# A second combine with a home for every tile's rows, summed on TensorE through diagonals of the weights

## The reference, cut to what matters

```
# expert FFN (64 experts, 6 chosen per token, at most 64 tokens per expert; later ones are dropped)
scores = softmax(xf @ gate_w.T);  topk_w, topk_idx = top_k(scores, 6)
eo = (silu(g) * u) @ down_proj * buf_w;  routed[token] += eo;  x = x + 0.5 * (routed + shared)
# wave FFN, on layernorm(x)
amp = sigmoid(x @ amp_w + amp_b);  ph = tanh(x @ ph_w + ph_b) * pi
h = (cos(ph) + sin(ph)) * amp
for l in range(2):
    e = h @ ent_w[l] + ent_b[l];  ent = e @ ent_pw[l] + ent_pb[l]
    h = layer_norm(h + ent, ln3_g[l], ln3_b[l])
    t = h @ path_w[l] + path_b[l]                    # two paths
    mod = cos(phase[l]) + sin(phase[l])
    h = layer_norm(h + sum over paths of t * mod, ln4_g[l], ln4_b[l])
```

## Time and profile before

| | us |
|---|---|
| median of 3 runs | 786.45 (785.43 to 788.97) |
| profiled execution | 787.34 |
| its span | 785.7 |
| PE / DVE / ACT / POOL busy | 577.7 / 389.2 / 233.4 / 295.2 |
| 48 gathers of the second combine (L1610), POOL busy | 51.3 |
| input wave's products (L1814), PE | in groups of 4 tiles |

### The profile page before, as it was taken

The page is one execution under the profiler, slowest core; times in us unless marked ns, Lnnn a source line. Parts: engine busy times, 40 slices in busy tenths (PEclk is TensorE's granted clock), DMA queues, the critical chain, the costliest instruction groups (busy, mean ns, idle before and its releaser), DMA issues. The chain is left out here.

```text
span 785.7 us, 10359 instructions
## 1 busy us (share of the span) xinstructions
PE 577.7 (74%) x3486; PEld 368.9 (47%) x3486; DVE 389.2 (50%) x1102; ACT 233.4 (30%) x638; POOL 295.2 (38%) x383
## 2 busy tenths in 40 slices
PE   2666259970799999998953398984336697897796
PEld 1334125530466666665632254564213586554485
DVE  4656213333475676855442033366758547624135
ACT  1222024440132232321310144420033463142664
POOL 0556611106601537160326012257754266003065
PEclk9757569995799999998985599987577798998899
DMA  8886048842200314340166168733370000000001
GB/s 322 290 295 215 16 129 271 282 164 80 73 9 1 81 41 85 35 170 4 37 241 138 55 211 301 243 104 98 89 80 1 0 1 1 1 1 0 2 1 53
DMA packets 39723, 82.96 MB, mean 106 GB/s; under 512 B 7805, under 2 KB 27906, under 8 KB 38816
## 3 DMA queue, kind: packets, MB, share of 16 engines
q1 hardware_dynamic: 26144, 45.03, 17.7%
q0 software_dynamic: 13248, 37.07, 17.2%
q10 hardware_dynamic: 288, 0.30, 0.1%
HBM read 60.21 MB, written 26.35 MB: 110 GB/s over the span
## 5 line engine op out<-in xcount | busy, mean ns | idle before, releaser
L434 POOL DMA_INDIRECT expert_in<-xn_sent,scatter_slots x72 | 70.9, 985 | 79.7 <-DVE slots L383 50.5
L770 DVE SCALAR_TENSOR_TENSOR work<-work,banks 128x96 f32<-128x96 f32 x64 | 16.3, 254 | 124.1 <-ACT work L750 124.1
L1845 PE MATMUL banks<-w_gu,w_dn 128*128 128x256 f32 x256 | 68.4, 394 | 0.0
L1610 POOL DMA_INDIRECT w_dn<-expert_out,slots x48 | 51.3, 1069 | 26.4 <-issue 14.2
L790 PE MATMUL banks<-ident,work 128*128 128x128 f32 x128 | 29.5, 316 | 42.6 <-DMA work<-expert_in 42.6
L1251 POOL DMA_INDIRECT w_gu<-expert_out,gather_slots x48 | 49.3, 1028 | 28.7 <-DVE gather_slots L1259 14.7
L799 PE MATMUL banks<-w_gu,work 128*64 128x192 f32 x512 | 58.5, 352 | 0.0
L1968 POOL TENSOR_TENSOR var_eps<-mv,eps 128x1 f32<-128x1 f32 (+1 forms) x70 | 13.7, 195 | 116.8 <-ACT w_dn L1894 55.2
L1845 PEld LDWEIGHTS banks<-w_gu,w_dn 128*128 128x128 f32 x256 | 46.0, 199 | 4.2
L790 PEld LDWEIGHTS banks<-ident,work 128*128 128x128 f32 x128 | 13.8, 149 | 67.5 <-issue 41.5
L1970 POOL TENSOR_TENSOR rstd<-var_eps,minus_half 128x1 f32<-128x1 f32 (+1 forms) x70 | 42.4, 606 | 5.5
(11 more groups left out here) (271 smaller groups left out, 1258.0 us busy)
## 6 DMA issues: line engine op xcount, KB each, us to landing
work<-expert_in SPq DMA_DIRECT2D x64, 128.0 KB, 3.8
expert_out<-work SPq DMA_DIRECT2D x64, 128.0 KB, 3.8
w_gu<-in_gate_up SPq DMA_DIRECT2D x10, 768.0 KB
w_gu<-in_gate_up POOLq DMA_DIRECT2D x6, 768.0 KB, 5.6
expert_in<-w_dn SPq DMA_DIRECT2D x4, 1024.0 KB, 7.5
w_dn<-in_down SPq DMA_DIRECT2D x10, 384.0 KB
w_gu<-in_gate_up SPq DMA_DIRECT2D x1, 3840.0 KB, 12.0
w_dn<-in_down SPq DMA_DIRECT2D x1, 3072.0 KB, 25.8
```

The source lines that it names most:

```text
L434: nc.gpsimd.indirect_dma_start(out=m.expert_in, out_offset=bass.IndirectOffsetOnAxis(m.scatter_slots[u][:, at:at + 1], 0), in_=xn[:, t, :] ...
L1610: nc.gpsimd.indirect_dma_start(out=w.combined[q % 2][:, t * TOPK + k, :], out_offset=None, in_=m.expert_out, in_offset=bass.IndirectOffset ...
L1845: last = nc.tensor.matmul(f.p_lin[t % DEEP], f.uT[t % DEEP][:, c, :], w.lin[:, step, c, :], start=(step > 0 and c == 0), stop=(c == KC - 1))
```

## The change

Every tile has a home for its 6 x 256 gathered columns (`w.combined`, eight places; tile 7 takes tile 0's), so gathers no longer wait for a buffer's combine. ACT makes a diagonal matrix of each tile's weights for each choice (8 places), PE sums the six products of diagonal and rows into PSUM bank 2 or 3, and DVE adds the bank to `m.x`. `fold_phase` and `last_phase` become one block. The input wave runs in groups of tiles 0 to 3, 4 and 5, 6 and 7 (`FIRST_NORM`), each with its own root on POOL: the first behind the gathers of tile 5, the second behind those of tile 6, the third at the end. `finish_maps` and the attention's weights (`finish_qkv`) move ahead of the last tiles. The phases are reduced by POOL in the second expert stage (`phases_to_turns`, ahead of `load_last_weights`), with two loads of its own. The first wave's transpositions use two banks, so a transposition waits for the copy of the tile two before it; the wait is there in the second wave too.

```diff
@@ experts_phase, call 1, POOL @@
+                phases_to_turns(nc, m, a, pool, x.out, before)
                 for part, groups_used in enumerate((2, 3, 4, 6), 1):
+def phases_to_turns(nc, m, a, pool, s_out, before):
...
+    pool.dma_start(w.phase, a["rows"][:, first:first + NL * PW * D].broadcast_to([P, NL * PW * D])).then_inc(m.s_phase, 16)
+    pool.dma_start(w.ent_b.rearrange("p a b -> p (a b)"), a["ent_b"]).then_inc(m.s_phase, 16)
+    pool.wait_ge(m.s_phase, 32)
...
+    for l in range(NL):
...
+        chain(nc.gpsimd.tensor_scalar(turns, phase, 0.5 / PI, big, ALU.mult, ALU.add))
+        chain(nc.gpsimd.tensor_scalar(whole, turns, -big, None, ALU.add))
+        for part in (c1, c2):
+            chain(nc.gpsimd.tensor_scalar(turns, whole, -part, None, ALU.mult))
+            chain(nc.gpsimd.tensor_tensor(phase, phase, turns, ALU.add))
+        chain(nc.gpsimd.tensor_scalar(turns, phase, TURN_PI, -TURN_PI, ALU.min, ALU.max))
+    pool.wait_ge(s_out, before + RING)
+    for l in range(NL):
+        chain(nc.gpsimd.tensor_copy(w.ent_b_wide[:, l], w.ent_b[:, l, :].unsqueeze(2).broadcast_to([P, EW // P, P])))
@@ finish_maps, on DVE @@
     split_bias(nc, m, w, chain)
+    meanwhile()
     for k in range(1, STEPS):
         eng.wait_ge(s_last, k)
...
+def fold_pool(nc, m, w, s, wave, pool):
+    last_row = pool.to_reg(SLOTS + P - 1)
+    for t in range(TILES):
+        if t == 6:
+            pool.wait_ge(s.sin, 2 * NL)
+        if t == 7:
+            pool.wait_ge(s.summed, 1)
+        for k in range(TOPK):
+            nc.gpsimd.indirect_dma_start(
...
+                bounds_check=last_row, oob_is_err=False).then_inc(s.gathered[t], 16)
+        if t == 5:
+            norm_roots_pool(nc, m, wave, pool, 0, [0])
+        if t == 6:
+            norm_roots_pool(nc, m, wave, pool, 0, [1])
+    norm_roots_pool(nc, m, wave, pool, 0, [2])
+def fold_scalar(nc, m, w, f, s, wave, act):
+    def diagonals(t):
+        for k in range(TOPK):
...
+            nc.scalar.activation(w.diag[j % DIAGS], m.ident[:, :], ACT.Copy, scale=m.weights[:, t, k:k + 1]
+                                 ).then_inc(s.diag, 1)
...
+    for t in range(5):
+        diagonals(t)
+    wave_scalar_x(nc, w, f, wave, act, 0, range(0, 4))
+    diagonals(5)
+    wave_scalar_x(nc, w, f, wave, act, 0, range(4, 6))
+    diagonals(6)
+    diagonals(7)
+    wave_scalar_x(nc, w, f, wave, act, 0, range(6, 8))
+def fold_vector(nc, m, w, f, s, wave, dve, chain):
+    def add_sum(t):
+        dve.wait_ge(s.summed, t + 1)
+        chain(nc.vector.tensor_tensor(m.x[:, t, :], m.x[:, t, :], m.banks[:, 2 + t % 2, 0:D], ALU.add))
+        dve.sem_inc(s.added, 1)
...
+    add_sum(0)
+    add_sum(1)
...
+    finish_maps(nc, m, w, dve, chain, s.maps, s.scaled, s.last_steps, lambda: (add_sum(2), add_sum(3)))
+    stats_all_vector(nc, m, wave, chain, range(0, 4))
+    apply_all_vector(nc, m, f, wave, dve, 0, range(0, 4))
+    add_sum(4)
+    add_sum(5)
+    stats_all_vector(nc, m, wave, chain, range(4, 6))
+    dve.wait_ge(s.small, 4 * 16)
+    finish_qkv(nc, w, chain)
+    apply_all_vector(nc, m, f, wave, dve, 0, range(4, 6))
+    for t in range(6, 8):
+        add_sum(t)
+        stats_all_vector(nc, m, wave, chain, range(t, t + 1))
+    apply_all_vector(nc, m, f, wave, dve, 0, range(6, 8))
+def fold_tensor(nc, m, w, f, s, wave, pe):
+    def sum_tile(t):
+        if t >= 1:
+            pe.wait_ge(s.added, t)
+        for k in range(TOPK):
...
+            pe.wait_ge(s.diag, j + 1)
+            last = nc.tensor.matmul(m.banks[:, 2 + t % 2, 0:D], w.diag[j % DIAGS], w.combined[t][:, k, :],
+                                    start=(k == 0), stop=(k == TOPK - 1))
...
+    pe.wait_ge(s.halved, 1)
+    nc.tensor.matmul(m.banks[:, 3, :], w.last_row, w.amp_ph[:, KC - 1, :], start=True, stop=True).then_inc(s.last, 1)
+    pe.wait_ge(m.s_ent, 16 * 2 * NL)
...
+    sum_tile(0)
+    sum_tile(1)
+    for k in range(1, STEPS):
+        step_shift(k)
+    sum_tile(2)
+    sum_tile(3)
+    pe.wait_ge(s.scaled, 1)
...
+    sum_tile(4)
+    wave_tensor_x(nc, m, w, f, wave, pe, 0, range(0, 4), f.p_turn_x)
+    sum_tile(5)
+    wave_tensor_x(nc, m, w, f, wave, pe, 0, range(4, 6), f.p_turn_x)
+    sum_tile(6)
+    sum_tile(7)
+    wave_tensor_x(nc, m, w, f, wave, pe, 0, range(6, 8), f.p_turn_x)
@@ wave_tensor_x @@
         if p < tiles.stop:
+            if p >= 2:
+                eng.wait_ge(s.xT, norms * TILES + (p - 1))
```

More of the change, by code:

```diff
@@ L1477, in last_weights @@
     w.parts = [g[:, first:first + 128].bitcast(BF16) for first in (8192, 8960, 3072)]
-    w.combined = [flat(d, 10240 + 3072 * b, (TB * TOPK, D)) for b in range(2)]
+    one = TOPK * D
+    homes = [d[:, 10240 + one * b:10240 + one * (b + 1)] for b in range(4)]
+    homes += [m.work[:, 0:one], m.work[:, one:2 * one], m.w_qkv[:, :, :].rearrange("p c n -> p (c n)"), homes[0]]
+    w.combined = [home.rearrange("p (k d) -> p k d", d=D) for home in homes]
+    spare = m.w_qkv[:, :, :].rearrange("p c n -> p (c n)")
+    w.phase = spare[:, 0:NL * PW * D]
+    w.turns = [spare[:, 2 * PW * D:3 * PW * D], m.w_proj[:, :, :].rearrange("p c n -> p (c n)")]
+    w.cos_turns = [tile[:, :, :].rearrange("p t d -> p (t d)") for tile in (m.xn, m.xn_sent)]
+    w.ent_b = flat(m.w_sgu[:, :, :].rearrange("p c n -> p (c n)"), 0, (NL, EW // P))
     return w
@@ new lines, with __init__ @@
+class Fold:
+    def __init__(self, sem):
+        self.small = sem("small_last_weights_loaded")
+        self.prod, self.read = sem("fold_product_ready"), sem("fold_products_read")
+        self.wide = sem("bias_columns_spread")
+        self.halved, self.last = sem("amplitude_map_halved"), sem("last_row_of_input_maps_ready")
+        self.abs, self.sin, self.half = sem("phase_sizes_ready"), sem("phase_sines_ready"), sem("half_pi_made")
+        self.gathered = [sem(f"last_rows_gathered_tile{t}") for t in range(TILES)]
+        self.diag, self.used = sem("weight_diagonal_ready"), sem("weight_diagonal_used")
+        self.summed, self.added = sem("tile_summed"), sem("tile_sum_added")
+        self.maps, self.scaled, self.last_steps = sem("step_maps_ready"), sem("step_maps_scaled"), sem("last_row_of_step_maps_ready")
@@ new lines, in fold_scalar @@
+def fold_scalar(nc, m, w, f, s, wave, act):
+    def diagonals(t):
+        for k in range(TOPK):
+            j = t * TOPK + k
+            if j >= DIAGS:
+                last_used = j - DIAGS
+                if last_used % TOPK == TOPK - 1:
+                    act.wait_ge(s.summed, last_used // TOPK + 1)
+                else:
+                    act.wait_ge(s.used, last_used - last_used // TOPK + 1)
+            nc.scalar.activation(w.diag[j % DIAGS], m.ident[:, :], ACT.Copy, scale=m.weights[:, t, k:k + 1]
+                                 ).then_inc(s.diag, 1)
+    for l in range(NL):
+        nc.scalar.activation(w.cos_turns[l], w.turns[l], ACT.Abs).then_inc(s.abs, 1)
+    act.wait_ge(s.half, 1)
+    act.wait_ge(s.abs, NL)
+    for l in range(NL):
+        both = slice(l * PW, (l + 1) * PW)
+        nc.scalar.activation(w.phase_sin[:, both].rearrange("p a b -> p (a b)"), w.turns[l], ACT.Sin).then_inc(s.sin, 1)
+        nc.scalar.activation(w.phase_cos[:, both].rearrange("p a b -> p (a b)"), w.cos_turns[l], ACT.Sin, scale=-1.0,
+                             bias=w.half_pi).then_inc(s.sin, 1)
+    for t in range(5):
[6 more added lines that the diff above has]
+    wave_scalar_x(nc, w, f, wave, act, 0, range(6, 8))
@@ L2044, in _ @@
         def _(pe):
-            def last_rows():
-                pe.wait_ge(s_scaled, 1)
-                pe.wait_ge(wave.tanh, TILES)
-                for k in range(1, STEPS):
-                    nc.tensor.matmul(m.banks[:, 4 + k, 0:D], w.last_row, w.lin[:, k, KC - 1, :], start=True, stop=True
-                                     ).then_inc(s_last, 1)
-            wave_tensor(nc, m, w, f, wave, pe, 0, s_maps, REST, last_rows)
+            fold_tensor(nc, m, w, f, fold, wave, pe)
+            wave_tensor(nc, m, w, f, wave, pe, 0, fold.maps)
             for t in range(TILES):
```

337 lines of the change are left out of this document (140 added, 197 removed).

## The result

The changed kernel takes 800.38 us (median of 8 runs, 793.41 to 811.82) against 788.04 (785.43 to 789.34) for the kernel before on the same chip: 1.0128 times the time [1.0095, 1.0162]. The forecast of 788.0, with a range to 793.5, was wrong. Besides being slower, it scatters: 18 us from lowest to highest where before scatters by 4. Its mean granted clock was 0.874 in the run of 793.41 us and 0.841 in that of 811.82.

What follows compares the result with a forecast made beforehand. Bound: the stretch from 516 to 616 us, where no engine is busy throughout and POOL's gather issues are the backbone. Terms +0.3 (first step), +0.4 (second wave), +0.9 (crowded loads) gave +1.6: 788.0 on the median, range 780.5 to 793.5.

Steps and rivals of the forecast that it cites:

- Phases: Second expert stage: POOL's arithmetic takes up to 20 us, moves the first load 0 to 5 us; crowding costs 0.9.
- The loads crowd: Rival, chance 0.23: the first megabyte load comes at 466 with the second, the expert stage loses some 4 more: 792.
- an expert stage longer by over 2 us: Sign of being wrong: the expert stage takes over 2 us longer than in the kernel before.
- The load at the start: New 512 KB load, starting with the second expert stage: lands some 5.2 us later, POOL free between 446 and 466.
- Maps ready: DVE's step maps in the fold: 15.2 us in all, done at 566.4.
- the first root: POOL's root ahead of tile 6's gathers: waits for statistics at 568.1, POOL idle 1 to 2 us before it.
- sum 5: Tile 5's sum on TensorE: comes behind the wave of tiles 0 to 3, which ends at 582.3.
- the gathers of tile 7: POOL, behind the second root: issued from about 588, the sixth at 595.4, landed at 599.4.
- first step: First transposition of the steps on TensorE, end of the fold: 616.1 against 615.77 before.
- The gate: First root stands in POOL's program ahead of tile 6's gathers and waits for 568.1, with 12 gathers queued behind it.
- The clock stays high: Rival, chance 0.26: idle stretches do not lower TensorE's clock, the four-tile wave takes 10.2 instead of 12.5: -6.5, 781.5.
- Gathers starve: Rival, chance 0.10: DVE's scalings lengthen the first 36 gathers by at most 4 us, ending at 570.7: 790.6.

Runs made afterwards that it cites:

- the repeat: The changed kernel measured once more, unedited: 799.73 us, 1.0164 times the kernel before.
- e1: Changed kernel with POOL's 16 phase instructions dealt out between the loads of the last weights: 791.98 us, 1.0073 times the kernel before.
- e8: e1 with POOL's 512 KB load held until the second expert stage's second pair is out: 787.2 us, 1.0015 times the kernel before.
- e6: e5 with the second root of the input wave behind tile 7's gathers in POOL's program: 789.87 us, 1.0029 times the kernel before.
- e7: e5 with tile 5's sum ahead of one six-tile wave, tiles 4 and 5 normalised before the attention fold: 780.8 us, 0.9922 times before.
- e11: Changed kernel with the 512 KB load held until the second pair is out, arithmetic left in one block: 794.74 us, 1.0128 times before.
- e2: Kernel before, with POOL waiting until the second expert stage's 12th pair ahead of the first load of last weights: 792.26 us, 1.0089.
- e5: Changed kernel with phase reductions and spreads back on DVE in the fold, the 512 KB load gone: 790.99 us, 1.0043 times before.

## Why the prediction was wrong

**The step that failed is *Phases*.** Its upper end of 20 us for the arithmetic met the 19.8 measured by luck: ten of the 14 instructions took 1.27 to 1.53 us, above the 1.13 that stood for the dearest case, and the two spreads together 2.13 instead of 4.5. Of the 0 to 4 us that crowded loads might cost I took 0.9, near the lower end, because the later loads are paced by the experts. They are (473.86 and on, 4 us apart); the first three had come due meanwhile and left together (in the repeat, two). And the bound of 4 us counted only waits on rows: the waits hardly changed, and the price came as 24 us at half clock behind one late pair, 10.4 in all. A cost bounded by how long an engine waits left out what its clock does afterwards. The rival *The loads crowd* named mechanism and condition (POOL's last spread ending behind 461; it ended at 467.5) and had 0.23; its price of some 4 us more was short by the same term. The sign that the prediction gave for being wrong, an expert stage longer by over 2 us, is the one that came. The load at the start, which the step let pass as landing 5.2 us later, adds the wait of pair 1 that e1 and e8 show; it is not in the first profile of after, but in the repeat (2.17 us).

**The rest held**, each with the stage's 11.1 us taken off. Maps ready 565.7 (forecast 566.4); POOL idle 3.4 us ahead of the first root (1 to 2; the gathers came 1.33 us apart, not 1.40) and 9.0 ahead of the second (about 9); tiles normalised from 569.2 (569.8); sum 5 begun at 581.3 (behind 582.3); the gathers of tile 7 from 587.0 (588); sum 7 ended at 602.6 (603.2); first step 615.8 (616.1; the terms as written add up to 616.0). The fold is 99.16 against 99.18.

***The gate* was half right.** It does delay tile 7's rows, but e6 takes it away and gains 0.4 us of fold: the sums' place in the programs of TensorE and ScalarE binds by itself. The prediction's own sum says so, with tile 7's rows landed at 599.4 and the sum of tile 6 until 600.5; that POOL's wait "gives all of it back" does not follow from it. What gives the tail's gain back is the order, with the sum of tile 5 behind the wave of tiles 0 to 3; e7 changes it and gets 9.9 us. The forecast of the fold was right with this cause misnamed.

**The other rivals** are out. *The clock stays high*: it was 0.50 ahead of the first wave here too, and the wave of four tiles took 11.7 us (580.28 to 591.98), between the forecast's 12.5 and this rival's 10.2:

```profile
578.00:581.00 3.00, 0.25 (x1) 0.25 (x2) 1.44 (x9) 0.00 (x0) 1.88 (x3) 0.50 0.01 3
```

*Gathers starve*: beside the maps' scalings they took 1000 ns at the median and 1118 at most, and eight of DVE's twelve scalings 398 ns at the median, 406 in before, though the longest took 523 for 408. All twelve together took 4.8 us for 4.5. The lock between the two engines that the Trainium skill ("SBUF — State Buffer", Who interferes with whom) describes costs 0.3 us at most in this stretch.

```profile
L1640 POOL DMA_INDIRECT work<-expert_out,slots x12: 994/1000/1118, 559.8 to 574.4; - x12
```

## What to carry to other kernels

Work moved to an idle engine takes the time of that engine's queue: look up what stands behind it, and deal the moved instructions out between paced transfers rather than ahead of them. Price a late operand not by the wait alone but by the clock that may follow it. Before removing a wait, ask which instruction would be late next in program order; here it was the order, not the wait.

## What was not expected of the hardware

- The granted clock stayed at 0.50 for 24 and 27 us with TensorE busy all the time (24.00 of 24.00), behind waits of 1.90 and 1.66 us, and for some 10 us behind 1.51; behind waits of 2.38 (e11) and 2.27 (e2) it did not fall. What decides stays open.
- POOL's operation of 128x512 by a number took 0.61 us as multiplication and addition, 1.5 as one of them alone, 1.92 to 1.94 as two additions. The Trainium skill ("GPSIMD Engine Reference", Engine selection) gives twice VectorE's time for two inputs and calls one input "roughly line-rate". The trace agrees on two inputs (1.27 against DVE's 0.69); with one, POOL took 0.61 to 1.94, by the form, where DVE took 0.43 in e5.
